# Normalizing x of batches 1 to 3 on ScalarE instead of the vector engine, in a fused attention and mixture-of-experts kernel

## Chip, cores and metric

The kernel runs on one core of one Trainium2 chip. The metric is the device time of one execution in microseconds (us). Engines are named as in the profile: PE is TensorE's matmul, PEld its weight load, DVE is VectorE, ACT is ScalarE, POOL is GpSimd, SP is SyncE.

## The reference, cut to what matters

```python
x = L0_attn_x                                     # (4, 2048, 256) float32
x = x + _layernorm(_L0_attn_ref(_layernorm(x), Wqk, Wv, Wo, tau))
x = x + _layernorm(_L0_ffn_ref(_layernorm(x), ln_g, ln_b, Wr, W1, W3, W2, W1s, W3s, W2s))

def _layernorm(x, eps=1e-5):
    return (x - mean(x)) / sqrt(var(x) + eps)     # over the last axis
def _L0_attn_ref(x, Wqk, Wv, Wo, tau):            # attention over channels
    qk, v = heads_of(x @ Wqk), heads_of(x @ Wv)   # 16 heads of 16 channels, transposed to (b, h, d, n)
    dot = einsum('bhdn,bhen->bhde', qk, qk)
    ...
```

The attention is over channels: its logits come from `dot`, which is Wqk^T (x^T x) Wqk with x the normalized input. So the kernel needs, for each of the 4 batches, one Gram matrix x^T x of 256x256, summed over 2048 tokens. The feed-forward part has one shared expert over all tokens and 7 routed ones, top 2, with a capacity. All is float32.

## The kernel before

**Tiling.** Tokens are cut into 16 groups of 512 (four a batch, `q` = 0 to 3), each held as `[128, GT=4, 256]`. The feed-forward part is a stream of chunks of 512 tokens: `first_chunks()` gives the shared expert's chunks 0 to 13, `routed_chunks` the routed ones, `held_chunks` the last two. Float32 products are made of three fp32r ones: every operand is split into a high part, a rounded copy made by ACT, and a low part, the difference, made by DVE. `three(...)` issues the three matmuls (L1140 to L1142).

**A chunk.** `body` on each engine runs eight steps `m` per chunk. PE: `up` (L1323) makes two products of 512 columns, six matmuls each, into bank 0 and bank 1; `down` for an earlier step (L1345) takes twelve matmuls of 256 columns. ACT: SiLU from bank 0 into `sb_act` (L1063), then the high part of the step before (L1034). DVE: the multiply of bank 1 with `sb_act` (L1738), then the low part (L1714). In chunks 0 to 11 one pair of banks serves: the first six matmuls of the next `up` wait for the SiLU, its other six for the multiply.

**What sets the order.** Each engine has one instruction stream in program order, with semaphores between them. The attention of batches 1 to 3 is threaded by hand into this stream: step m of chunk n has two places, 16n+2m and 16n+2m+1, and `put` enters steps in `schedule` at places. `attend` issues on each engine what that engine has under the step's name (`steps`). On ACT the even place lies behind the SiLU and ahead of the high part, the odd one behind the high part and ahead of the next SiLU. On DVE the even place lies behind the multiply and ahead of the low part, the odd one ahead of the next multiply.

```python
X_STEPS = (("x_stats", 0), ("x_norm", 3), ("x_high", 4), ("x_part", 5))
...
X_AT, M_AT, MIX_AT = (None, 14, 72, 131), (None, 34, 93, 152), (None, 46, 109, 164)
for b in range(1, B):
    ...
    for q in range(GB):
        put(b, X_AT[b] + 4 * q, q, X_STEPS)
```

So `x_norm` stands at places 17, 21, 25, 29 of batch 1, at 75, 79, 83, 87 of batch 2 (odd places), and at 134, 138, 142, 146 of batch 3 (even places).

**The steps around the change.** For group q: `x_stats` on DVE takes mean and variance of `xin` into `mvX` (L1431, L1435, L1449); POOL makes `rstdX` (L780); `x_norm` on DVE (L1451, its instructions L1460) writes (x - mean) * rstd to `xnorm[q % 2]`, which is the tile `sb_xn` or `sb_ln_o`, in four instructions of 256 columns; `x_high` on ACT (L930, L933) writes its high part into `xx` (the tiles `sb_wdn_hi` and `sb_wdn_lo`, idle weight space), `x_part` on DVE (L1565, L1568) its low part; `x_gram` on PE (L1144, L1159) multiplies them. When `xn_ok` rises, SP loads the next tokens into `xin` (L560), or the turned x (L570), which ACT splits in `x_keep` (L939). Other steps in the same stretch: `o_add` on DVE (L1584) adds the attention's result, `u_norm` on DVE (L1608, L1612) normalizes for the router, `u_turn0` and `u_turn1` on ACT (L988) copy transposed rows to `sb_hr`, `prep` copies `sb_hfull` to `sb_h_hi` (L1015).

Of the kernel before, what the change touches and what calls it, by code (L numbers as in the profile page):

```python
# [7 lines left out]
ALU = mybir.AluOpType  # L8
ACT = mybir.ActivationFunctionType
# [7 lines left out]
P = 128  # L17
# [4 lines left out]
OPEN = 4  # L22
# [23 lines left out]
def sandwich_kernel(nc, x_in, Wqk, Wv, Wo, tau, ln_g, ln_b, Wr, W1, W3, W2, W1s, W3s, W2s, x_turned, out):  # L46
# [10 lines left out]
    GT = 4  # L57
# [3 lines left out]
    GB = N // GW  # L61
# [36 lines left out]
    with ExitStack() as ctx:  # L98
        def sb(name, shape, dt=F32):
            return ctx.enter_context(nc.sbuf_tensor("sb_" + name, shape, dt))  # L100

        def sem(name):
            return ctx.enter_context(nc.semaphore(name))
# [39 lines left out]
        xin = sb("xin", [P, 2, GT, D])  # L143
        xn = sb("xn", [P, GT, D])
        ln_o = sb("ln_o", [P, GT, D])
        xnorm = [xn, ln_o]
# [38 lines left out]
        stX = sb("stX", [P, 2, GT, 6])  # L185
        mvX = sb("mvX", [P, 2, GT, 2])
        rstdX = sb("rstdX", [P, 2, GT])
        veX = sb("veX", [P, GB, GT])
        outidx = sb("outidx", [P, NG], U32)
        stB = sb("stB", [P, GT, 6])  # L190
# [69 lines left out]
        a_rstd = sem("a_rstd")  # L260
        xn_ok = sem("xn_ok")
        xn_tile = sem("xn_tile")
        xhi_ok = sem("xhi_ok")
        xlo_ok = sem("xlo_ok")
        xT_in = [sem(f"xT_in{i}") for i in range(GB)]
# [2 lines left out]
        g_done = sem("g_done")  # L268
# [658 lines left out]
        def _(act_e):  # L927
            s = nc.scalar

            def x_high(b, q):  # L930
                act_e.wait_ge(xn_ok, OPEN + b * GB + (q + 1))
                act_e.wait_ge(g_done, OPEN + b * GB + q - 1)
                s.activation(xx[q % 2][:, :, 0, :], xnorm[q % 2][:, :, :], ACT.Copy).then_inc(xhi_ok, 1)  # L933
# [22 lines left out]
            def m_halves(dst, banks, ready, order):  # L956
                def step(b, q):
                    for n, k in enumerate(order):
                        act_e.wait_ge(m_pe, b * MP + ready + n)
                        s.activation(dst[:, k, :], bank[banks[k]][:, 0:D], ACT.Copy).then_inc(m_act, 1)  # L960
                return step
# [11 lines left out]
            def u_keep(k):  # L973
                def step(b, q):
# [10 lines left out]
                    if opens(b, q):  # L985
# [3 lines left out]
                                 scale=gcol[:, k:k + 1], bias=bcol[:, k:k + 1]).then_inc(hT_ok, 1)  # L989
                return step  # L990

            steps = {"x_high": x_high, "x_keep": x_keep, "m_gram": m_gram,
                     "m_keep_t": m_halves(tsb, (5, 4), 2, (1, 0)),
                     "m_exp": m_step(lc[:, :, :], lc[:, :, :], m_dve, 3, ACT.Exp),
                     "m_keep_n": m_halves(tsb, (6, 5), 6, (0, 1)),
# [132 lines left out]
            for t in range(GT // 2):  # L1128
                ins = s.activation(last_y[CLOSE % TY][:, t, :], last_y[CLOSE % TY][:, t, :], ACT.Identity,
                                   scale=t_scale[CLOSE % SLOTS][:, t:t + 1], bias=t_bias[CLOSE % SLOTS][:, t:t + 1])  # L1130
# [293 lines left out]
        def _(dve):  # L1424
            v = nc.vector
# [12 lines left out]
            def x_from(b, q):  # L1438
                return x2[:, q, :, :] if b == 0 and q < 2 else xin[:, q % 2, :, :]
# [11 lines left out]
            def x_norm(b, q):  # L1451
                g = b * GB + q
                dve.wait_ge(a_rstd, g + 1)
                if g < GB + 2:
                    dve.wait_ge(g_done, OPEN + g - 1)
                else:
                    dve.wait_ge(xhi_ok, OPEN + g - GB - 1)
                    dve.wait_ge(xlo_ok, OPEN + g - GB - 1)
                for t in range(GT):
                    ins = v.tensor_scalar(xnorm[q % 2][:, t, :], x_from(b, q)[:, t, :], mvX[:, q % 2, t, 0:1],  # L1460
                                          rstdX[:, q % 2, t:t + 1],
                                          ALU.subtract, ALU.mult)
                    if b == 0 and t < GT - 1:
                        ins.then_inc(xn_tile, 1)
                ins.then_inc(xn_ok, 1)

# [198 lines left out]
            def u_place(b, pair):  # L1665
# [17 lines left out]
                dve.sem_inc(r_slot, 1)  # L1683

            steps = {"x_stats": x_stats, "x_norm": x_norm, "x_part": x_part, "x_low": x_low, "o_add": o_add,
                     "m_turn": m_sum, "m_sym": m_sym, "m_pick": m_pick, "m_logits": m_logits,
                     "m_softmax": m_softmax, "m_low": m_low, "o_stats": o_stats, "o_norm": o_norm,
                     "u_stats": u_stats, "u_norm": u_norm, "u_turn1": first_keep, "u_copy": u_copy, "r_top": r_top, "r_next": r_next,
                     "u_slot": u_slot, "u_place": u_place}
# [175 lines left out]
            for t in range(GT // 2, GT):  # L1865
                ins = v.tensor_scalar(y[:, t, :], y[:, t, :], t_scale[CLOSE % SLOTS][:, t:t + 1], t_bias[CLOSE % SLOTS][:, t:t + 1],
                                      ALU.mult, ALU.add)
# [40 lines left out]
```

## Time and profile before

| | before |
|---|---|
| median of 3 runs | 1089.29 us (1087.91 to 1089.88) |
| the profiled execution's own time | 1087.53 us |
| its span | 1085.8 us |
| PE busy / PEld busy | 1049.2 us (97%) / 958.5 us (88%) |
| DVE busy | 656.1 us (60%) |
| ACT busy | 503.5 us (46%) |
| POOL busy | 390.0 us (36%) |
| TensorE clock granted, mean | 0.993 |

The span is the time from the first to the last instruction of one profiled execution; the execution's own time has some 1.7 us around it. Busy time of an engine is the union of its instructions; matmuls overlap one another, so PE can be busy while it is not at its peak. A timeline row gives an instruction's start, its length, and in brackets how long its engine had been idle before it and what ended that.

### The profile page before, as it was taken

How to read it: one execution, taken by the hardware profiler on the slowest of the kernel's cores; microseconds unless marked ns; L12 is line 12 of the kernel's file. 1: busy time of each engine (PE TensorE's matmuls, PEld its weight loads, DVE VectorE, ACT ScalarE, POOL GpSimd, SP SyncE). 2: the span in 40 equal slices, each digit the busy share in tenths (PEclk: the TensorE clock that was granted, in tenths of full speed). 3: DMA queues.
4: the chain of work that ended last, by engine and by line, in shares of the span. 5: the costliest groups of instructions: out<-in, count | busy, mean ns of one | idle time of the engine just before them, and what ended most of it. 6: DMA issues, size and time to landing. Idle time of an engine off the chain costs nothing.

```text
span 1085.8 us, 19513 instructions
## 1 busy us (share of the span) xinstructions
PE 1049.2 (97%) x6863; PEld 958.5 (88%) x6863; DVE 656.1 (60%) x1714; ACT 503.5 (46%) x895; POOL 390.0 (36%) x347
## 2 busy tenths in 40 slices
PE   7998999999999999999989999999999999999995
PEld 6886888888888988889878899999999999999874
DVE  7768864677754578754786334545545463635686
ACT  4343344443434444443454334554546463645485
POOL 3112661114640114541116731344443343312386
PEclk9999999999999999999999999999999999999998
DMA  8322460242540223461134214524344342333699
GB/s 280 114 98 78 138 214 20 78 157 93 174 142 20 100 96 141 134 221 49 59 136 162 93 43 152 139 62 117 82 96 106 68 124 52 81 79 105 239 237 178
DMA packets 47229, 129.15 MB, mean 119 GB/s; under 512 B 10276, under 2 KB 17576, under 8 KB 47152
## 3 DMA queue, kind: packets, MB, share of 16 engines
q1 hardware_dynamic: 28656, 92.83, 25.1%
q0 software_dynamic: 18496, 35.35, 14.2%
q8 instruction: 43, 0.70, 0.3%
q14 instruction: 34, 0.28, 0.1%
HBM read 73.72 MB, written 54.40 MB: 118 GB/s over the span
## 4 chain that ended last, share of the span: by engine, by line
PE 82%; DVE 8%; POOL 3%; issue 3%; ACT 1%; DMA 1%; DVEq 0%; SPq 0%; POOLq 0%; ACTq 0%
PE bank L1140 25%; PE bank L1142 25%; PE bank L1141 25%; PE bank L1159 3%; POOL out_dram L908 2%; POOL sb_place_of L913 2%; DVE sb_act L1738 1%; PE bank L1266 1%; PE bank L1319 1%; DVE sb_act_lo L1714 1%; PE bank L1219 1%; DVE sb_stX L1431 1%; DVE sb_st L1431 1%; PE bank L1278 1%; ACT sb_ln_o L967 1%
## 5 line engine op out<-in xcount | busy, mean ns | idle before, releaser
L1140 PE MATMUL bank<-sb_h_hi,sb_wup_lo 128*128 128x512 f32 (+2 forms) x960 | 354.4, 369 | 5.3 <-DVE sb_act L1738 3.8
L1738 DVE TENSOR_TENSOR sb_act<-bank,sb_act 128x512 f32<-128x512 f32 (+2 forms) x240 | 148.6, 619 | 345.9 <-PE bank L1142 317.1
L1142 PE MATMUL bank<-sb_h_hi,sb_wup_hi 128*128 128x512 f32 (+2 forms) x960 | 350.0, 365 | 0.0
L1141 PE MATMUL bank<-sb_h_lo,sb_wup_hi 128*128 128x512 f32 (+2 forms) x960 | 349.6, 364 | 0.0
L1063 ACT ACTIVATE sb_act<-bank 128x512 f32<-128x512 f32 (+2 forms) x240 | 129.8, 541 | 354.6 <-PE bank L1142 328.9
L1140 PE MATMUL bank<-sb_wdn_hi,sb_act_lo 128*128 128x256 f32 (+1 forms) x848 | 246.5, 291 | 5.8 <-DVE sb_act_lo L1714 5.8
L1142 PE MATMUL bank<-sb_wdn_hi,sb_act_hi 128*128 128x256 f32 (+1 forms) x848 | 240.1, 283 | 0.0
L1141 PE MATMUL bank<-sb_wdn_lo,sb_act_hi 128*128 128x256 f32 (+1 forms) x848 | 239.9, 283 | 0.0
L1140 PEld LDWEIGHTS bank<-sb_h_hi,sb_wup_lo 128*128 128x128 f32 x960 | 180.5, 188 | 27.2 <-DVE sb_act L1738 6.4
L1142 PEld LDWEIGHTS bank<-sb_h_hi,sb_wup_hi 128*128 128x128 f32 x960 | 180.5, 188 | 22.5
L1141 PEld LDWEIGHTS bank<-sb_h_lo,sb_wup_hi 128*128 128x128 f32 x960 | 180.9, 188 | 17.0
L1140 PEld LDWEIGHTS bank<-sb_wdn_hi,sb_act_lo 128*128 128x128 f32 (+1 forms) x848 | 159.7, 188 | 11.6 <-DVE sb_act_lo L1714 6.9
L1714 DVE TENSOR_TENSOR sb_act_lo<-sb_act,sb_act_hi 128x512 fp32r<-128x512 f32 (+2 forms) x240 | 147.2, 613 | 36.1 <-ACT sb_act_hi L1034 34.8
L1141 PEld LDWEIGHTS bank<-sb_wdn_lo,sb_act_hi 128*128 128x128 f32 (+1 forms) x848 | 159.6, 188 | 3.3
L1142 PEld LDWEIGHTS bank<-sb_wdn_hi,sb_act_hi 128*128 128x128 f32 (+1 forms) x848 | 159.5, 188 | 0.0
L1034 ACT ACTIVATE sb_act_hi<-sb_act 128x512 fp32r<-128x512 f32 (+2 forms) x240 | 136.6, 569 | 0.3 <-DVE sb_act L1738 0.3
L864 POOL DMA_INDIRECT y_scratch<-sb_ysb,sb_scur x42 | 76.9, 1832 | 154.1 <-ACT sb_ysb L1052 87.8
L784 POOL TENSOR_TENSOR sb_rstdB<-sb_veB,sb_mhalf 128x4 f32<-128x4 f32 x16 | 19.0, 1187 | 218.1 <-DVE sb_veB L1557 218.1
L800 POOL DMA_INDIRECT sent_scratch<-sb_rows,sb_sendto x64 | 70.7, 1104 | 28.9 <-issue 19.9
L833 POOL DMA_INDIRECT sb_rows<-sent_scratch,sb_gcur x42 | 44.6, 1063 | 77.3 <-issue 52.5
L788 POOL TENSOR_TENSOR sb_rstd<-sb_ve,sb_mhalf 128x4 f32<-128x4 f32 x16 | 19.8, 1239 | 77.5 <-DVE sb_ve L1593 77.5
L967 ACT ACTIVATE sb_ln_o<-bank,sb_nbiasB,sb_rstdB 128x256 f32<-128x256 f32 x64 | 30.9, 563 | 27.5 <-DVE sb_nbiasB L1562 27.5
(265 smaller groups left out, 1240.6 us busy)
## 6 DMA issues: line engine op xcount, KB each, us to landing
sb_xin<-in_L_ffn_W_dram SPq DMA_DIRECT2D x28, 512.0 KB, 3.5
sb_x<-in_L_attn_x_dram SPq DMA_DIRECT2D x16, 512.0 KB, 3.7
out_dram<-sb_x SPq DMA_DIRECT2D x16, 512.0 KB, 3.5
sb_xin<-in_L_attn_x_dram SPq DMA_DIRECT2D x14, 512.0 KB, 5.1
sb_xin<-in_x_turned_dram SPq DMA_DIRECT2D x14, 512.0 KB, 3.9
y_scratch<-sb_ysb SPq DMA_DIRECT2D x14, 512.0 KB, 3.6
sb_xn<-in_L_ffn_W_dram SPq DMA_DIRECT2D x14, 512.0 KB, 3.9
hT_scratch<-sb_hr SPq DMA_DIRECT2D x12, 512.0 KB
```

Of the source, the lines that this page charges most:

```text
L800: pool.indirect_dma_start(sent_d, bass.IndirectOffsetOnAxis(ap=sendto[:, q, t, c:c + 1], axis=0), u[q][:, t, :], None).then_inc(sent[q], 16)
L833: pool.indirect_dma_start(rows[0:w, part, t, :], None, sent_d, bass.IndirectOffsetOnAxis(ap=gcur[0:w, part, t:t + 1], axis=0)).then_inc(ga ...
L864: pool.indirect_dma_start(y_d, bass.IndirectOffsetOnAxis(ap=scur[0:w, par, part, t:t + 1], axis=0), ysb[0:w, part, t, :], None, compute_op ...
L967: ins = s.activation(ln_o[:, t, :], bank[o_bank(b, q) + t // 2][:, (t % 2) * D:(t % 2 + 1) * D], ACT.Identity, scale=rstdB[:, t:t + 1], bi ...
L1034: s.activation(act_hi[:, m % 4, 0:c.w], act[:, m % 3, 0:c.w], ACT.Copy).then_inc(ahi_ok, 1)
L1063: s.activation(act[:, m % 3, 0:c.w], a[:, 0:c.w], ACT.Silu).then_inc(silu_ok, 1)
L1140: t_.matmul(o, a_lo, b_hi, start=start, stop=False, skip_group_check=True)
L1141: t_.matmul(o, a_hi, b_lo, start=False, stop=False, skip_group_check=True)
L1142: return t_.matmul(o, a_hi, b_hi, start=False, stop=stop, skip_group_check=True)
L1159: ins = t_.matmul(bank[4 + k][:, o:c], a[:, k * P:(k + 1) * P], a[:, o:c], start=(q == 0 and t == 0), stop=(q == GB - 1 and t == GT - 1))
L1714: v.tensor_tensor(act_lo[:, m % 4, 0:c.w], act[:, m % 3, 0:c.w], act_hi[:, m % 4, 0:c.w].bitcast(F32), ALU.subtract).then_inc(alo_ok, 1)
L1738: v.tensor_tensor(act[:, m % 3, 0:c.w], bank[(4 if c.wide and m % 2 else 0) + 1][:, 0:c.w], act[:, m % 3, 0:c.w], ALU.mult).then_inc(act_o ...
```

## The change

On DVE, `x_norm` of batches 1 to 3 no longer writes the normalized tile; it makes the four bias values per partition, -mean * rstd, in one small instruction and signals `x_nb`. On ACT a new `x_norm`, at the same places of the schedule, waits for it and writes the tile by four ACTIVATEs with scale rstd and that bias. Its wait for the tile to be free is the old one (`g_done` or `xlo_ok`); `xhi_ok` is no longer waited for, since `x_high` is earlier on the same engine. Batch 0 is as it was. Instructions per group: DVE loses four of 128x256 and gains one of 128x4, ACT gains four of 128x256; there are 12 groups.

```diff
+        nbX = sb("nbX", [P, 2, GT])
...
+        x_nb = sem("x_nb")
...
+            def x_norm(b, q):
+                if b == 0:
+                    return
+                g = b * GB + q
+                act_e.wait_ge(x_nb, g - GB + 1)
+                if g < GB + 2:
+                    act_e.wait_ge(g_done, OPEN + g - 1)
+                else:
+                    act_e.wait_ge(xlo_ok, OPEN + g - GB - 1)
+                for t in range(GT):
+                    ins = s.activation(xnorm[q % 2][:, t, :], xin[:, q % 2, t, :], ACT.Identity,
+                                       scale=rstdX[:, q % 2, t:t + 1], bias=nbX[:, q % 2, t:t + 1])
+                ins.then_inc(xn_ok, 1)
...
-            steps = {"x_high": x_high, "x_keep": x_keep, "m_gram": m_gram,
+            steps = {"x_norm": x_norm, "x_high": x_high, "x_keep": x_keep, "m_gram": m_gram,
...
             def x_norm(b, q):
                 g = b * GB + q
                 dve.wait_ge(a_rstd, g + 1)
-                if g < GB + 2:
-                    dve.wait_ge(g_done, OPEN + g - 1)
-                else:
-                    dve.wait_ge(xhi_ok, OPEN + g - GB - 1)
-                    dve.wait_ge(xlo_ok, OPEN + g - GB - 1)
+                if b > 0:
+                    v.scalar_tensor_tensor(out=nbX[:, q % 2, :], in0=mvX[:, q % 2, :, 0], scalar=-1.0,
+                                           in1=rstdX[:, q % 2, :], op0=ALU.mult, op1=ALU.mult).then_inc(x_nb, 1)
+                    return
+                dve.wait_ge(g_done, OPEN + g - 1)
                 for t in range(GT):
                     ins = v.tensor_scalar(xnorm[q % 2][:, t, :], x_from(b, q)[:, t, :], mvX[:, q % 2, t, 0:1],
                                           rstdX[:, q % 2, t:t + 1],
                                           ALU.subtract, ALU.mult)
-                    if b == 0 and t < GT - 1:
+                    if t < GT - 1:
                         ins.then_inc(xn_tile, 1)
                 ins.then_inc(xn_ok, 1)
```

How the streams now stand (the lines of the changed kernel are 16 higher from L946 on). ACT in batch 1, from the first group's place on; before, `sb_act<-bank0` is the SiLU, `sb_wdn_hi1` and `sb_wdn_lo1` are `x_high`:

```order
L1034 ACTIVATE sb_act_hi<-sb_act 128x512
L1063 ACTIVATE sb_act<-bank0 128x512
L933 ACTIVATE sb_wdn_hi1<-sb_xn 128x4x256
L1034 ACTIVATE sb_act_hi<-sb_act 128x512
L1063 ACTIVATE sb_act<-bank0 128x512
L1034 ACTIVATE sb_act_hi<-sb_act 128x512
L1045 ACTIVATE sb_ysb<-bank2 128x512
L1045 ACTIVATE sb_ysb<-bank3 128x512
L1063 ACTIVATE sb_act<-bank0 128x512
L933 ACTIVATE sb_wdn_lo1<-sb_ln_o 128x4x256
```

The same stretch now, where `sb_xn<-sb_xin` and `sb_ln_o<-sb_xin` are the new `x_norm`:

```order
L1050 ACTIVATE sb_act_hi<-sb_act 128x512
L942 ACTIVATE sb_xn<-sb_xin,sb_nbX,sb_rstdX 128x256 x4
L1079 ACTIVATE sb_act<-bank0 128x512
L949 ACTIVATE sb_wdn_hi1<-sb_xn 128x4x256
L1050 ACTIVATE sb_act_hi<-sb_act 128x512
L1079 ACTIVATE sb_act<-bank0 128x512
L1050 ACTIVATE sb_act_hi<-sb_act 128x512
L1061 ACTIVATE sb_ysb<-bank2 128x512
L1061 ACTIVATE sb_ysb<-bank3 128x512
L942 ACTIVATE sb_ln_o<-sb_xin,sb_nbX,sb_rstdX 128x256 x4
L1079 ACTIVATE sb_act<-bank0 128x512
L949 ACTIVATE sb_wdn_lo1<-sb_ln_o 128x4x256
```

Four ACTIVATEs now stand directly ahead of a SiLU, in both groups; before, the SiLU stood ahead of everything that needs the normalized tile. DVE at the first of these two places, now (L1600 is `o_add`, L1754 the multiply):

```order
L1730 TENSOR_TENSOR sb_act_lo<-sb_act,sb_act_hi 128x512
L1600 TENSOR_TENSOR sb_x2<-sb_ln_o,sb_x2 128x1024
L1471 SCALAR_TENSOR_TENSOR sb_nbX<-sb_mvX,sb_rstdX 128x4
L1754 TENSOR_TENSOR sb_act<-bank1,sb_act 128x512
L1675 TENSOR_TENSOR sb_place_of<-bank6,sb_carry 128x112
```

The bias stands where the four DVE instructions stood, behind `o_add` and ahead of the multiply. ACT in batch 3 at its first group's place, now:

```order
L1079 ACTIVATE sb_act<-bank0 128x512
L942 ACTIVATE sb_xn<-sb_xin,sb_nbX,sb_rstdX 128x256 x4
L1050 ACTIVATE sb_act_hi<-sb_act 128x512
L1004 ACTIVATE sb_hr<-bank6,sb_bcol,sb_gcol 128x512
L949 ACTIVATE sb_wdn_hi1<-sb_xn 128x4x256
L1079 ACTIVATE sb_act<-bank0 128x512
```

Here the new step stands behind a SiLU; ahead of the next SiLU come the high part, the copy to `sb_hr` and `x_high`, as before, but now all behind the four ACTIVATEs.

## Rows read from the trace of the kernel before

**Rows 1.** The page, busy time of each engine over the span.
```profile
PE 1049.2 (97%) x6863; PEld 958.5 (88%) x6863; DVE 656.1 (60%) x1714; ACT 503.5 (46%) x895; POOL 390.0 (36%) x347
```
**Rows 2.** Waits of PE from 80 to 560 us: us in total, times, longest.
```profile
PE bank L1140 <- DVE sb_act L1738: 3.5, 3, 2.8
...
PE bank L1159 <- DVE sb_wdn_lo L1568: 0.3, 1, 0.3
```
**Rows 3.** Line L1460 from 60 to 560 us: who waited for it (us, times).
```profile
  ACT sb_wdn_lo L933: 12.4, 4
  ACT sb_wdn_hi L933: 7.1, 3
```
**Rows 4.** Timeline of ACT near the end, start and length in us.
```profile
1030.30 1.08 ACT L1114 ACTIVATE sb_xn<-sb_xn,sb_place_of 128x256 f32<-128x256 f32 x2
```
**Rows 5.** Line L1562 of DVE, the bias of another layer norm, ns min/median/max.
```profile
L1562 DVE SCALAR_TENSOR_TENSOR sb_nbiasB<-sb_mvB,sb_rstdB x16: 151/152/161, 40.5 to 546.9; 128x4 f32<-128x4 f32 x16
```
**Rows 6.** Timeline of all engines, batch 1, groups 0 and 1.
```profile
97.40 0.60 ACT L1063 ACTIVATE sb_act<-bank 128x512 f32<-128x512 f32 x1 [0.82 <-DVE sb_act_lo L1714]
...
98.36 1.38 DVE L1460 TENSOR_SCALAR sb_xn<-sb_xin,sb_mvX,sb_rstdX 128x256 f32<-128x256 f32 x4
98.43 0.39 PE L1140 MATMUL bank<-sb_h_hi,sb_wup_lo 128*128 128x512 f32 x1
...
99.65 0.69 DVE L1738 TENSOR_TENSOR sb_act<-bank,sb_act 128x512 f32<-128x512 f32 x1
...
106.89 0.68 DVE L1738 TENSOR_TENSOR sb_act<-bank,sb_act 128x512 f32<-128x512 f32 x1
...
107.62 0.50 PE L1140 MATMUL bank<-sb_h_hi,sb_wup_lo 128*128 128x512 f32 x1 [2.75 <-DVE sb_act L1738]
...
111.59 1.37 DVE L1460 TENSOR_SCALAR sb_ln_o<-sb_xin,sb_mvX,sb_rstdX 128x256 f32<-128x256 f32 x4
...
114.15 0.39 PE L1140 MATMUL bank<-sb_h_hi,sb_wup_lo 128*128 128x512 f32 x1
```
**Rows 7.** Busy time by stretch: PE, PEld, DVE, ACT, POOL, granted clock, DMA share, GB/s.
```profile
104.60:108.00 3.40, 0.65 (x4) 0.34 (x3) 3.19 (x11) 0.60 (x2) 1.91 (x1) 1.00 0.41 165
108.00:111.40 3.40, 3.40 (x13) 2.92 (x12) 3.04 (x10) 0.00 (x0) 1.19 (x1) 0.50 0.01 2
```
**Rows 8.** Timeline of all engines, batch 1, group 3.
```profile
131.21 0.60 ACT L1063 ACTIVATE sb_act<-bank 128x512 f32<-128x512 f32 x1 [3.09 <-PE bank L1142]
...
133.45 1.38 DVE L1460 TENSOR_SCALAR sb_ln_o<-sb_xin,sb_mvX,sb_rstdX 128x256 f32<-128x256 f32 x4
...
137.08 1.22 DVE L1470 TENSOR_TENSOR sb_wup_lo<-sb_xin,sb_wup_hi 128x1024 fp32r<-128x1024 f32 x1
...
138.22 1.22 DVE L1568 TENSOR_TENSOR sb_wdn_lo<-sb_ln_o,sb_wdn_lo 128x1024 fp32r<-128x1024 f32 x1
...
138.75 1.06 ACT L939 ACTIVATE sb_wup_hi<-sb_xin 128x1024 fp32r<-128x1024 f32 x1 [0.46 <-DMA sb_xin<-in_x_turned_dram]
...
140.31 1.81 PE L1159 MATMUL bank<-sb_wdn_lo 128*128 128x512 f32 x8
```
**Rows 9.** Timeline of all engines, batch 2, group 1.
```profile
268.24 1.38 DVE L1460 TENSOR_SCALAR sb_ln_o<-sb_xin,sb_mvX,sb_rstdX 128x256 f32<-128x256 f32 x4
...
270.60 0.69 DVE L1738 TENSOR_TENSOR sb_act<-bank,sb_act 128x512 f32<-128x512 f32 x1 [0.98 <-PE bank L1142]
...
276.39 1.91 PE L1159 MATMUL bank<-sb_wdn_lo 128*128 128x512 f32 x8 [0.26 <-DVE sb_wdn_lo L1568]
```
**Rows 10.** Timeline of all engines, batch 3, group 0.
```profile
418.30 1.38 DVE L1460 TENSOR_SCALAR sb_xn<-sb_xin,sb_mvX,sb_rstdX 128x256 f32<-128x256 f32 x4 [0.25 <-DVE sb_sendto L1680]
...
420.68 0.58 ACT L1063 ACTIVATE sb_act<-bank 128x512 f32<-128x512 f32 x1
...
421.16 0.77 ACT L988 ACTIVATE sb_hr<-bank,sb_bcol,sb_gcol 128x512 f32<-128x512 f32 x1
421.31 0.50 PE L1140 MATMUL bank<-sb_h_hi,sb_wup_lo 128*128 128x512 f32 x1
```

## The prediction

> **What bounds the kernel now.** I read the page first: TensorE is busy for 97% of the span, DVE for 60%, ACT for 46% [rows 1]. So neither DVE nor ACT is short of time on the whole; a shift of work between them counts only where TensorE stands still for one of them. The second view is what TensorE waits for in the stretch with batches 1 to 3: the multiply L1738 holds it 3.5 us in 3 times, 2.8 of them at once, and the low part of normalized x (L1568) holds it 0.3 us in batch 2, group 1 [rows 2]. The third is the line that moves: ACT waited 12.4 + 7.1 = 19.5 us for its result [rows 3]. The last is the timeline at the twelve places, which decides.
>
> **Prices.** DVE loses, per group, four instructions that together take 1.38 us [rows 6], and gains one of 128x4, 0.15 us [rows 5]. ACT gains four ACTIVATEs from SBUF to SBUF, 128x256, with scale and bias per partition. The trace has this form at L1114: two take 1.08 us, and one alone 0.59, so they start 0.49 us apart [rows 4]. Four take 4 x 0.49 = 1.97 us until the next can start (the one alone is estimated as 1.08 - 0.49). The Trainium skill (page "VectorE: DVE Perf Modes", section "The TRN2 errata") has a table that gives ScalarE from SBUF to SBUF 224 + 256 cycles at 1.2 GHz, 0.40 us for one such instruction; by it a group would cost ACT some 1.6 us, each SiLU would be 0.4 us less late, and the sum below about 3.7 us. The rows say 0.59, and the measurement decides.
>
> ACT's 12 x 1.97 = 24 us are more than DVE's 12 x 1.2 = 15 us. Neither total is the change in time. What matters is the order: the four ACTIVATEs wait for DVE's bias, and the SiLU waits behind them, though it needs nothing of them. TensorE's next `up` needs that SiLU in its first six matmuls, and DVE's multiply, which stands right behind the bias, needs it too.
>
> **Batch 1, group 0.** The bias stands where the normalization started, 98.36, so it ends at 98.51. A hand-over takes some 0.05 us: the multiply that ends at 107.57 is followed by its matmul at 107.62 [rows 6]. ACT: 98.55 + 1.97 = 100.52, then the SiLU, 0.60, to 101.12. Before, the SiLU ran at 97.40 and its matmul at 98.43; now that matmul starts at 101.15, 2.7 us later. The multiply, before at 99.65, starts at 101.15 too, 1.5 later. From there to the multiply at 106.89 DVE has no pause (3.19 us busy of 3.40 in the stretch from 104.6, and all that it does there it does one after another [rows 7]), so TensorE's matmul at 107.62, which waits for that multiply, comes **1.5 us later**, not 2.7: DVE was the late one there and gets its own relief of 1.2 back only as a pause.
>
> **Group 1.** Its bias comes on DVE at 111.59 + 1.5 = 113.09. ACT: 113.28 + 1.97 = 115.25, SiLU to 115.85, and the matmul that waits for it at 115.9; before 114.15 [rows 6]. That is **+1.75** in all. The granted clock fell to half speed (1.2 of 2.4 GHz) from 108.0 to 111.4, behind a pause of 2.75 us [rows 7]; the new pause there is shorter (estimated 2.1 us), so the clock may hold. Worth nothing here: at full clock TensorE would be back at about 115.3 and still wait for the SiLU.
>
> **Groups 2 and 3.** Group 2 costs nothing: its SiLU comes late too, but TensorE has the router's matmuls and a Gram product in front of it. Group 3 does cost. Its bias stands at 133.45 behind a full DVE; the SiLU that ran at 131.21 now waits: 133.45 + 1.75 = 135.2, ACT from 135.4 to 137.4, SiLU to 138.0. Behind it on ACT stand the split of turned x (0.96 each, estimated as 1.06 less the overlap), `x_high` (the same) and a high part (0.52), to 140.4. Then DVE makes a low part (0.6), L1470 and L1568 (1.13 each) and ends at 143.4. Before, L1568 ended at 139.44 and the Gram product ran at 140.31 [rows 8]; now it starts at 143.45. So batch 1 costs **+3.1 us**. The DMA of turned x, which starts when the tile is written, is 2.6 us later and lands at about 141.3 instead of 138.75 [rows 8]; ACT's next split waits for it a little, with slack behind.
>
> **Batch 2.** Groups 0 and 2: DVE is not late there, the bias comes while TensorE still fills the SiLU's bank, and ACT's 1.97 us fit ahead of it: 0. Group 1: bias 268.24, ACT to 270.4, SiLU to 271.0, multiply 271.05 instead of 270.60, 0.45 later, and DVE then runs without a pause to L1568, for which the Gram product at 276.39 had waited already [rows 9]: **+0.45**. Group 3 by the same sum: **+0.3**.
>
> **Batch 3.** Even places: the step is behind a SiLU, so the high part comes late first, which has time. But the next SiLU stands behind all of it. Group 0: bias 418.30, ACT 418.5 to 420.46, high part 0.52 (as long as a SiLU, 0.6), copy to `sb_hr` 0.69 (0.77), `x_high` 0.97 (1.06), each less 0.1 of overlap, SiLU 422.64 to 423.22, matmul 423.27 instead of 421.31 [rows 10], nearly 2.0, of which some 0.25 are had back, since the next six matmuls had waited for DVE before. **+1.7**. Groups 1 to 3 together **+0.3** (the multiply behind group 2 comes late).
>
> **Where relief is.** The stalls that a freer DVE could shorten are those of rows 2. In the sum it shortens none, since each DVE queue has its multiply behind a SiLU that is later by more than DVE gains. I cost at nothing: the new semaphore, the dropped wait for `xhi_ok`, and SP's loads (the tile is done up to 2.6 us later; what they load is needed a group's step later). POOL has no new work.
>
> **Sum.** 3.1 + 0.75 + 2.0 = 5.85 us on the profiled execution's own 1087.53 us: 1093.4. The median of the runs is 1.76 us above that execution; 1089.29 + 5.85 gives **1095.1 us**. Bounds: the lower is what only the three first-order delays give, 1.5 + 1.7 = 3.2, less the scatter of the runs (1.4): 1091. The upper adds the clock (below).
>
> **Rivals.**
> 1. *The clock falls twice more.* TensorE would now stand for some 2.6 us at 98.6 and 2.0 us at 421.2; a pause of 2.75 us was followed by 3.4 us at half speed, which costs 1.7 us [rows 7]. Price up to 3.4 us on top: 1098.5. Against it: in batch 1 DVE's queue sets the end anyway.
> 2. *Faster: DVE is what TensorE waits for.* The mechanism is one: at 106.89 the multiply comes 1.2 us earlier, the pause of 2.75 us becomes 1.5, the clock does not fall (1.7 us), the 0.4 of the first multiply and the 0.6 of L1568 go: about 4.5 us, 1084.8. For it: DVE ends nearly all of TensorE's waits here [rows 2]. It decides at one point: whether the bias is made before the SiLU could run. At 98 us the SiLU could run at 97.40 and the bias comes at 98.51 [rows 6]; at 131 it is 2.2 us before the bias [rows 8]. Only batch 2 has it the other way.
> 3. *No change: it fits in the time in which ACT waited.* ACT sat 19.5 us idle for this tile [rows 3] and now writes it itself; if TensorE's slack took the late SiLUs, the time stays 1089.3. For it: groups 0 and 2 of batch 2. Against: in batch 1 and 3 the matmul had 0.4 us or less behind the SiLU [rows 6, 10]: it ended at 98.00 and was used at 98.43.
> That the change does not do what it says can be left out: the streams show it.
>
> The Trainium skill (page "ScalarE: Activation LUTs", section "Rules for kernel authors") says to put additions and multiplications on VectorE, not ScalarE; the rows agree per instruction, 0.49 against 0.33 us apart, but by that rule alone the price would be 24 - 15 = 9 us, which no row supports, since neither engine is full.
>
> **How the numbers follow.** The forecast has 0.69, the clock rival 0.12, no change 0.10, faster 0.09. The range reaches from 1091.0 to 1099.0: the two rivals on the slower side are in it, the other two (0.19) are out. A measurement of this kernel tells 0.2%, 2.2 us, from no change. The forecast's own lower bound is above that, so slower has 0.69 + 0.12 = 0.81, within 0.2% 0.10, faster 0.09.
>
> **What would show it.** In the profile after: ACT's four ACTIVATEs start 0.2 us behind DVE's bias at some 98.5, 113.3, 135.4 and 420, with a SiLU right behind or behind three more; TensorE then has new waits for ACT's SiLU L1079 of about 2.6 us at 98.6, 0.5 at 115, 2.0 near 423, and one of 1 us for L1584 near 142. DVE's busy time falls by 15 us, ACT's rises by 24, ACT's waits of 19.5 us for the tile are gone. It is wrong if the SiLU at 98 us is not late, if four ACTIVATEs take far from 2 us, or if a stall at 107 us became shorter than 1.6 us.

## The result and the profile after

| | before | after | after, repeated |
|---|---|---|---|
| median of the runs beside each other | 1088.97 us | 1097.16 us (1095.79 to 1099.97) | 1096.01 us (1095.08 to 1096.82), before 1087.33 |
| ratio to before, 95% interval | | 1.0094 (1.0075 to 1.0113) | 1.0086 (1.0073 to 1.0099) |
| span of the profiled execution | 1085.8 us | 1098.2 us | 1093.3 us |

The change makes the kernel slower, by 8.2 us between the medians of the first comparison and by 8.7 in the second. The first ratio, 1.0094, is more than the medians of that comparison give (1.0075); in the second the two agree within 0.1%. On the 1089.29 us of the forecast the first ratio gives 1099.5 us, the second 1098.7. The forecast was +5.85 us and 1095.1, its range 1091.0 to 1099.0: the direction is right, the size is too small by a third (of 8.7 us) or more (10.2 us by the first ratio), and the first ratio's value lies just over the range.

On the page after, the numbers of instructions have moved as the streams say [rows 1 for before]: DVE has 36 fewer and is busy for 13.8 us less, ACT has 48 more and is busy for 23.0 us more.

```profile
span 1098.2 us, 19525 instructions
PE 1051.8 (96%) x6863; PEld 960.0 (87%) x6863; DVE 642.3 (58%) x1678; ACT 526.5 (48%) x943; POOL 386.6 (35%) x347
```

The costliest groups of ACT, apart by form, hold the new line. It has two rows, one for each buffer of normalized x:

```profile
L942 ACT ACTIVATE sb_ln_o<-sb_xin,sb_nbX,sb_rstdX 128x256 f32<-128x256 f32 x24 | 12.5, 590 | 23.4 <-DVE sb_nbX L1471 23.4
L942 ACT ACTIVATE sb_xn<-sb_xin,sb_nbX,sb_rstdX 128x256 f32<-128x256 f32 x24 | 12.5, 590 | 12.1 <-DVE sb_nbX L1471 12.1
```

ACT used to wait 19.5 us for DVE's finished tile [rows 3]; now it waits 35.5 us for DVE's bias, and everything behind it on ACT waits too. What TensorE waited for between 80 and 570 us (engine, what it waited for: us in total, times, the longest), to be held against [rows 2]:

```profile
PE bank L1156 <- ACT sb_act L1079: 6.4, 5, 2.6
PE bank L1156 <- DVE sb_act L1754: 2.5, 2, 2.1
PE bank L1205 <- DVE sb_u L1513: 2.1, 2, 1.0
PE bank L1175 <- DVE sb_wdn_lo L1584: 2.0, 2, 1.1
PE bank L1282 <- DVE sb_early L1628: 1.0, 1, 1.0
```

The waits for ACT's SiLU (L1079) are new but for 1.3 us, and so is most of the wait for the low part of x (L1584, before L1568). The timeline of batch 1, group 0, shows how the first arises: ACT, then DVE, then TensorE (start, length, instruction, and in brackets the idle time before it with what ended it).

```profile
98.05 0.64 ACT L1050 ACTIVATE sb_act_hi<-sb_act 128x512 fp32r<-128x512 f32 x1
100.65 2.07 ACT L942 ACTIVATE sb_xn<-sb_xin,sb_nbX,sb_rstdX 128x256 f32<-128x256 f32 x4 [1.97 <-DVE sb_nbX L1471]
102.63 0.57 ACT L1079 ACTIVATE sb_act<-bank 128x512 f32<-128x512 f32 x1
```

```profile
98.72 0.69 DVE L1730 TENSOR_TENSOR sb_act_lo<-sb_act,sb_act_hi 128x512 fp32r<-128x512 f32 x1 [2.52 <-ACT sb_act_hi L1050]
99.33 1.22 DVE L1600 TENSOR_TENSOR sb_x<-sb_ln_o,sb_x 128x1024 f32<-128x1024 f32 x1
100.46 0.15 DVE L1471 SCALAR_TENSOR_TENSOR sb_nbX<-sb_mvX,sb_rstdX 128x4 f32<-128x4 f32 x1
103.24 0.69 DVE L1754 TENSOR_TENSOR sb_act<-bank,sb_act 128x512 f32<-128x512 f32 x1 [2.62 <-ACT sb_act L1079]
```

```profile
103.26 0.50 PE L1156 MATMUL bank<-sb_h_hi,sb_wup_lo 128*128 128x512 f32 x1 [2.57 <-ACT sb_act L1079]
```

ACT is free at 98.7, DVE's bias comes at 100.6 behind a residual addition (L1600) that has nothing to do with it, the SiLU stands behind the four ACTIVATEs, and DVE then stands for 2.62 us for that SiLU. Each engine waits for the other in turn, and though neither is busy, TensorE's matmul comes 2.8 us later than before (103.26 for 98.43, less the 2.0 us that are explained next).

One part of the profiled difference of 12.4 us isn't the change's. In the first execution TensorE's matmuls start 2.0 us later than before's from 37 us on, ahead of every instruction that was changed. The repetition has nothing of it; there they start 0.6 us earlier than before's. The granted clock of the same stretch in the two, first execution and repetition (columns: us, busy time of PE, PEld, DVE, ACT, POOL, PEclk, DMA share, GB/s):

```profile
34.30:37.70 3.40, 3.40 (x18) 2.95 (x17) 2.08 (x4) 2.15 (x4) 0.00 (x0) 0.50 0.00 0
```

```profile
34.30:37.70 3.40, 3.22 (x27) 3.21 (x27) 3.40 (x7) 1.19 (x2) 0.00 (x0) 1.00 0.00 0
```

### The profile page after: what moved, and what is told of

The parts are those of the page before. It is cut to its first block, busy times and chain, and to the rows that moved or that the text cites. A ratio compares the mean times of both kernels' runs of the same rounds, so it can differ in the third digit from the quotient of the medians.

```text
span 1098.2 us, 19525 instructions
## 1 busy us (share of the span) xinstructions
PE 1051.8 (96%) x6863; PEld 960.0 (87%) x6863; DVE 642.3 (58%) x1678; ACT 526.5 (48%) x943; POOL 386.6 (35%) x347
## 4 chain that ended last, share of the span: by engine, by line
PE 76%; DVE 12%; issue 4%; POOL 3%; ACT 3%; DMA 1%; DVEq 0%; POOLq 0%; ACTq 0%; SPq 0%
PE bank L1156 24%; PE bank L1158 23%; PE bank L1157 23%; PE bank L1175 2%; POOL out_dram L910 2%; POOL sb_place_of L915 2%; DVE sb_act L1754 1%; DVE sb_stX L1447 1%; DVE sb_act_lo L1730 1%; PE bank L1282 1%; PE bank L1335 1%; DVE sb_st L1447 1%; PE bank L1235 1%; ACT sb_ln_o L983 1%; DMA sb_ysb<-in_L_ffn_W2s_dram 1%
## 5 line engine op out<-in xcount | busy, mean ns | idle before, releaser
L1754 DVE TENSOR_TENSOR sb_act<-bank,sb_act 128x512 f32<-128x512 f32 (+2 forms) x240 | 148.6, 619 | 357.3 <-PE bank L1158 311.5
L1079 ACT ACTIVATE sb_act<-bank 128x512 f32<-128x512 f32 (+2 forms) x240 | 129.6, 540 | 326.8 <-PE bank L1158 300.5
L1050 ACT ACTIVATE sb_act_hi<-sb_act 128x512 fp32r<-128x512 f32 (+2 forms) x240 | 136.5, 569 | 0.3 <-DVE sb_act L1754 0.3
L983 ACT ACTIVATE sb_ln_o<-bank,sb_nbiasB,sb_rstdB 128x256 f32<-128x256 f32 x64 | 30.9, 563 | 28.8 <-DVE sb_nbiasB L1578 28.8
```

Of the source, the lines that this page charges most:

```text
L983: ins = s.activation(ln_o[:, t, :], bank[o_bank(b, q) + t // 2][:, (t % 2) * D:(t % 2 + 1) * D], ACT.Identity, scale=rstdB[:, t:t + 1], bi ...
L1050: s.activation(act_hi[:, m % 4, 0:c.w], act[:, m % 3, 0:c.w], ACT.Copy).then_inc(ahi_ok, 1)
L1079: s.activation(act[:, m % 3, 0:c.w], a[:, 0:c.w], ACT.Silu).then_inc(silu_ok, 1)
L1754: v.tensor_tensor(act[:, m % 3, 0:c.w], bank[(4 if c.wide and m % 2 else 0) + 1][:, 0:c.w], act[:, m % 3, 0:c.w], ALU.mult).then_inc(act_o ...
```

## The experiments

Every kernel ran in 5 rounds beside the kernel before on its chip (before's medians: 1086.74 us in the first series, 1087.33 and 1087.39 in the others). Effects below are differences of medians; the intervals are of the ratio, and the two need not agree (for dve_signal 5.6 us and 4.5 us). Two theories stood against each other. **Order**: the loss comes from where the ACTIVATEs and the bias stand in two queues that wait for each other. **Engine time**: it comes from 24 us of added ACT work.

| kernel | median | effect | ratio, 95% interval |
|---|---|---|---|
| act_time | 1086.31 us | -0.4 | 0.9991 (0.9981 to 1.0002) |
| bias_only | 1087.86 | +1.1 | 1.0006 (0.9996 to 1.0015) |
| pool_bias | 1086.32 | -0.4 | 0.9997 (0.9987 to 1.0008) |
| behind_silu | 1090.55 | +3.8 | 1.0029 (1.0017 to 1.0040) |
| after_again | 1096.01 | +8.7 | 1.0086 (1.0073 to 1.0099) |
| only_b1 | 1091.00 | +3.7 | 1.0040 (1.0025 to 1.0055) |
| only_b3 | 1091.34 | +4.0 | 1.0039 (1.0027 to 1.0051) |
| bias_early | 1087.86 | +0.5 | 1.0005 (0.9994 to 1.0016) |
| dve_signal | 1092.97 | +5.6 | 1.0041 (1.0026 to 1.0056) |
| behind_silu_b3 | 1090.19 | +2.8 | 1.0018 (1.0006 to 1.0031) |
| before_late | 1088.08 | +0.7 | 1.0005 (0.9993 to 1.0018) |
| pool_late | 1087.24 | -0.2 | 0.9998 (0.9985 to 1.0011) |

### The ACTIVATEs alone, the wait alone

act_time is the kernel before with four ACTIVATEs of the same form per group at the new places on ACT, waiting for nothing of DVE's:

```diff
+            def x_norm(b, q):
...
+                for t in range(GT):
+                    ins = s.activation(xx[q % 2][:, t, 0, :], wo[:, t % 2, :], ACT.Identity,
+                                       scale=mhalf[:, 0:1], bias=mhalf[:, 1:2])
```

> The kernel before, DVE normalizing as before, and on ACT at the places of x_norm four ACTIVATEs of the same form on constant data that nothing waits for, with no wait for a bias. Order theory: ACT has the time free where it stands, the SiLU is late by 0.75 us at most, +0 to +1 us over before. Engine-time theory (24 us more on ACT are the price): +4 us or more.

bias_only is the changed kernel with the four ACTIVATEs left out:

```diff
-                for t in range(GT):
-                    ins = s.activation(xnorm[q % 2][:, t, :], xin[:, q % 2, t, :], ACT.Identity,
-                                       scale=rstdX[:, q % 2, t:t + 1], bias=nbX[:, q % 2, t:t + 1])
-                ins.then_inc(xn_ok, 1)
+                act_e.sem_inc(xn_ok, 1)
```

> The changed kernel, but ACT's x_norm only waits for the bias and signals; its four ACTIVATEs are left out, so x of batches 1 to 3 is not normalized (the Gram products take old data). Order theory (the cost is that each SiLU stands behind the bias and the 1.97 us of ACTIVATEs): the SiLU at 98 us is then late by 0.75 us only and the multiply behind it early by 0.45, so the time is that of the kernel before or some 1 us less, 1086 to 1089.5. Coupling theory (the wait for the bias alone costs most of it): 1092 or more.

Both run within 0.2% of before. The 48 ACTIVATEs cost nothing, so engine time falls; the waits for the bias alone cost little too (0.6 to 1.1 us, not clear of the scatter). Only the two together cost 8 us: the ACTIVATEs fit into ACT's idle time if they may run when ACT gets there, and don't when they begin late.

### The bias from another queue

In pool_bias GpSimd makes the bias right behind rstd, which it makes anyway; ACT's part is the changed kernel's, place for place.

```diff
+                if b > 0:
+                    pool.wait_ge(a_rstd, b * GB + (q + 1))
+                    v.tensor_tensor(nbX[:, q % 2, :], mvX[:, q % 2, :, 0], rstdX[:, q % 2, :], ALU.mult).then_inc(x_nb0, 1)
+                    pool.wait_ge(x_nb0, (b - 1) * GB + (q + 1))
+                    v.tensor_scalar(nbX[:, q % 2, :], nbX[:, q % 2, :], -1.0, None, ALU.mult).then_inc(x_nb, 1)
```

> The changed kernel with the bias made by POOL right behind rstd (two small instructions), so that ACT's x_norm stands at the same places but does not wait for DVE's queue. Order theory: only the 1.97 us on ACT are left ahead of the SiLU, the matmul at 98 us is 0.75 us late instead of 2.7, batch 1 costs 0 to 1 us, in all -1 to +2 us against before. Engine-time theory: as the change, +8 us.

The loss is gone. The same groups of ACT and the timeline of GpSimd and ACT at batch 1, group 0:

```profile
L948 ACT ACTIVATE sb_ln_o<-sb_xin,sb_nbX,sb_rstdX 128x256 f32<-128x256 f32 x24 | 12.4, 591 | 3.3 <-POOL sb_nbX L788 3.3
L948 ACT ACTIVATE sb_xn<-sb_xin,sb_nbX,sb_rstdX 128x256 f32<-128x256 f32 x24 | 12.4, 592 | 0.6 <-POOL sb_nbX L788 0.6
```

```profile
94.05 0.25 POOL L788 TENSOR_SCALAR sb_nbX<-sb_nbX 128x4 f32<-128x4 f32 x1
...
96.66 2.08 ACT L948 ACTIVATE sb_xn<-sb_xin,sb_nbX,sb_rstdX 128x256 f32<-128x256 f32 x4
98.63 0.59 ACT L1085 ACTIVATE sb_act<-bank 128x512 f32<-128x512 f32 x1
```

The bias is there at 94.3, and ACT has the SiLU at 98.63 instead of 102.63 (100.6 without the 2.0 us of the opening). It also shows what the relief of DVE is worth here: ACT does the whole normalization, DVE is 14.6 us less busy than before (641.5 against 656.1), and the time is before's; the interval leaves room for a gain of 1.4 us.

### One place earlier on DVE

bias_early leaves ACT as changed and only lets DVE make the bias one place sooner.

```diff
-        X_STEPS = (("x_stats", 0), ("x_norm", 3), ("x_high", 4), ("x_part", 5))
+        X_STEPS = (("x_stats", 0), ("x_bias", 2), ("x_norm", 3), ("x_high", 4), ("x_part", 5))
```

> The whole change, but DVE makes the bias one place earlier in its order (about 1.5 us of its queue), ahead of that place's other work; ScalarE's four ACTIVATEs stay where they are. If what costs is how late the bias comes out of DVE's queue, the waits of ScalarE for the bias (36 us in all in the changed kernel) fall by a third or more and most of the loss goes: +1 to +4 us over before instead of +8. If a bias by DVE costs by its being DVE's at all, or if the ACTIVATEs' own 1.97 us per group are what delays the SiLU, it stays at +7 us or more.

It runs within 0.2% of before: of 8.7 us, 0.5 are left. Its groups of ACT and DVE's timeline:

```profile
L942 ACT ACTIVATE sb_ln_o<-sb_xin,sb_nbX,sb_rstdX 128x256 f32<-128x256 f32 x24 | 12.5, 591 | 14.2 <-DVE sb_nbX L1471 14.2
L942 ACT ACTIVATE sb_xn<-sb_xin,sb_nbX,sb_rstdX 128x256 f32<-128x256 f32 x24 | 12.5, 592 | 4.3 <-DVE sb_nbX L1471 4.3
```

```profile
94.06 0.15 DVE L1471 SCALAR_TENSOR_TENSOR sb_nbX<-sb_mvX,sb_rstdX 128x4 f32<-128x4 f32 x1
96.66 0.69 DVE L1730 TENSOR_TENSOR sb_act_lo<-sb_act,sb_act_hi 128x512 fp32r<-128x512 f32 x1 [2.45 <-ACT sb_act_hi L1050]
```

The one place was worth much more than the 1.5 us I had put to it: between the two places DVE stands 2.45 us for ACT's high part (L1050). A bias behind that wait is late by the wait as well: it comes at 94.06 here and at 98.46 in the changed kernel (100.46 less 2.0). ACT still waits 18.5 us for the bias in all, about what it waited for the tile before, and the time is only 0.5 us over before's. behind_silu (below) waits only 10.8 us (7.4 + 3.4) and loses 3.8. So the sum of an engine's waits doesn't rank the cost; what stands behind them does.

### An empty signal in the bias's place

dve_signal is pool_bias, with ACT also waiting for a signal that DVE gives where the changed kernel makes the bias. DVE computes nothing.

```diff
                 if b > 0:
+                    dve.sem_inc(x_go, 1)
                     return
...
                 act_e.wait_ge(x_nb, g - GB + 1)
+                act_e.wait_ge(x_go, g - GB + 1)
```

> GpSimd makes the bias right behind rstd, as in pool_bias, which ran at before's time; but ScalarE waits, ahead of its four ACTIVATEs, for an empty signal that DVE gives at the place in its order where the changed kernel's DVE makes the bias. DVE computes nothing for x here. If the loss is the place in DVE's order and nothing else, this kernel loses as the changed one does: +8 to +9 us over before, with TensorE's pauses of 2.5 us at 101 us, 0.9 at 143, 1.1 at 280 and 1.9 at 427. If the loss came of the small instruction that computes the bias, or of ScalarE reading what DVE has just written, it stays within 2 us of before.

+5.6 us by the medians, 4.5 by the ratio (2.8 to 6.1): half to two thirds of the loss, without any work. Group 0 of batch 3 loses what it lost in the change: TensorE's waits for the SiLU are

```profile
PE bank L1164 <- ACT sb_act L1087: 4.0, 3, 1.8
```

of which 1.84 at 424.6. A half clock of 3.4 us at 425.5, which the repetition of the change doesn't have, costs some 1.2 us more. What I missed is mostly in batch 1: over it TensorE falls behind before's start times by 0.9 us here and by 3.3 in the change (over batch 2 by 0.4 and 1.2). In its group 0 ACT starts at 96.84, before DVE's addition begins, where in the change the bias came only after that addition:

```profile
96.84 2.08 ACT L950 ACTIVATE sb_xn<-sb_xin,sb_nbX,sb_rstdX 128x256 f32<-128x256 f32 x4 [0.25 <-issue]
```

```profile
96.62 0.69 DVE L1737 TENSOR_TENSOR sb_act_lo<-sb_act,sb_act_hi 128x512 fp32r<-128x512 f32 x1 [2.52 <-ACT sb_act_hi L1058]
97.23 1.22 DVE L1607 TENSOR_TENSOR sb_x<-sb_ln_o,sb_x 128x1024 f32<-128x1024 f32 x1
```

So a bare signal isn't a stand-in for an instruction at the same place: by 96.84 it had left DVE, when the low part ahead of it was still running and the addition was still to start. The kernel is a clean test of the place for batch 3, group 0, and not for batch 1; for batch 1 bias_early is the test.

### Behind the SiLU instead of ahead of it

behind_silu calls the ACTIVATEs at the head of `x_high`, one place later on ACT; in batches 1 and 2 this is behind the SiLU.

```diff
             def x_high(b, q):
+                x_norm(b, q)
...
-            steps = {"x_norm": x_norm, "x_high": x_high, "x_keep": x_keep, "m_gram": m_gram,
+            steps = {"x_high": x_high, "x_keep": x_keep, "m_gram": m_gram,
```

> The changed kernel with ACT's x_norm moved down one place, directly ahead of x_high: in batches 1 and 2 it then stands behind the SiLU, in batch 3 behind the high part and the copy to sb_hr, still ahead of the next SiLU. Same instructions on every engine. Order theory: batches 1 and 2 cost nothing and give back up to 1.5 us (DVE's relief at 98 to 107 us), batch 3 costs 0.75 us: 1087 to 1090.5. Engine-time theory: as the change, 1095 or more.

Batch 1 is healed. Up to 500 us the pauses of TensorE that are left over before's are three: 0.35 at 276.2 and 1.18 at 298.4 (batch 2, the low part of x, which now comes late), 0.8 at 423.6 (batch 3). The expectation had batch 2 at nothing. behind_silu_b3 moves batch 3 one place further:

```diff
-            steps = {"x_high": x_high, "x_keep": x_keep, "m_gram": m_gram,
+            steps = {"x_high": lambda b, q: b < 3 and x_high(b, q),
+                     "x_part": lambda b, q: b == 3 and x_high(b, q), "x_keep": x_keep, "m_gram": m_gram,
```

> behind_silu cost +3.1 us, and its trace has TensorE pauses grown by 0.8 us at 423.6 us (batch 3, where ScalarE's normalization still stood ahead of the next SiLU) and by 0.4 and 1.2 us in batch 2 (276 and 298 us). Here batch 3's stands one place later, behind the next SiLU. If the order against the SiLU is what costs, the pause at 423.6 us goes back to 0.1 us and the time falls to +2 to +2.5 us over before, the rest being batch 2's; if the later place makes a Gram product late instead, a new pause of 0.5 us or more stands in front of a product of x in batch 3, and the time stays at +3 or goes over it.

The pause at 423.6 went, and one of 0.39 for the low part appeared at 426.1; the gain (1.0 us by the medians measured beside before) is inside the intervals. A later place for the ACTIVATEs trades a late SiLU for a late Gram product.

### Batch by batch

> The changed kernel once more, beside the kernels of this series. Its first profiled execution was 12.4 us slower in its span than before's, of which 2.0 us arose at 32 to 36 us, ahead of anything that the change touches, behind a weight load that landed late, and 1.3 us came from a clock fall at 430.3 us. If the 2.0 us are scatter and the clock fall belongs to the change, this execution has no loss at 32 us and again a half clock of 3.4 us behind TensorE's pause at about 428 us, and the median is 8 to 9 us over before's. If the clock fall is scatter too, the median lies 6 to 7 us over before's. If the opening's loss belongs to the change, the median lies 10 us or more over.

> The change in batch 1 alone; batches 2 and 3 are normalized by DVE as before. The sum on record gives batch 1 +3.1 us, the changed kernel's trace +3.3: so +3 to +3.5 us over before, with pauses of about 2.6 us at 101 us and 2.1 us at 109 us and 0.9 us at 143 us. If the loss were not local but came of the engine time of all 48 ACTIVATEs, this one would cost a third of the whole change, 2.7 us, which the time alone can't tell apart, but then no pause of TensorE would have grown at these three places.

> The change in batch 3 alone. By the sum on record +2.0 us; if the pause of 1.9 us at its first group brings the clock down for 3.4 us, as in the changed kernel's trace, +1.8 for the pause, +1.3 for the clock and +0.7 for group 2: +3.8 us. A trace without a half clock between 420 and 430 us, with the time at +2 to +2.5 us, would say that the fall belongs to what batches 1 and 2 left behind.

Both single-batch kernels pick their batches by a list:

```diff
-                if b == 0:
+                if b not in MOVED:
                     return
...
-                if b > 0:
+                if b in MOVED:
                     v.scalar_tensor_tensor(out=nbX
```

Batch 1 alone costs 3.7 us, batch 3 alone 4.0, and of the 8.7 of both with batch 2 one us is left for it; batch 2 alone was not run. TensorE's start times, held against before's matmul for matmul, test this better than the medians. Over batch 1 they fall behind by 3.3 us in only_b1 and by 3.3 in the repetition, so batch 1's loss doesn't hang on the others. Over batch 3 they fall behind by 3.9 us in only_b3, 1.2 of them by a half clock, and by 2.3 in the repetition: 2.7 and 2.3 without the clock.

The repetition lost nothing at 32 us and had no half clock at 428 us, and its median is still 8.7 us over before's; the expectation had tied 8 to 9 us to that half clock.

The clock does not explain the loss of the profiled executions. Batch 3 alone had a clock fall behind its pause of 1.93 us, and so had the first execution of the whole change behind 1.94 us; the repetition had a pause of 1.95 us at the same place and no fall. Windows behind the pause in only_b3 and in the first execution, then two of the repetition (the second is the same place; columns as above):

```profile
425.10:428.50 3.40, 3.40 (x20) 2.26 (x22) 1.93 (x3) 0.60 (x1) 2.62 (x3) 0.50 0.65 258
```

```profile
430.30:433.70 3.40, 3.40 (x9) 2.63 (x9) 2.72 (x8) 1.52 (x3) 2.42 (x3) 0.50 0.87 343
```

```profile
102.00:105.40 3.40, 3.40 (x11) 2.75 (x10) 3.22 (x14) 1.21 (x3) 1.31 (x1) 0.50 0.95 311
427.60:431.00 3.40, 3.40 (x28) 2.42 (x28) 3.15 (x9) 1.60 (x3) 2.38 (x2) 1.00 0.93 376
```

Between 80 and 600 us the kernel before had two stretches of 3.4 us at half clock (108.0, 568.8), the change two (430.3, 580.4), its repetition two (102.0, 576.5). They moved; they did not become more. A fall did cost about 1.2 us where it came (TensorE's start times went from 2.36 to 3.55 us behind before's in only_b3, from 8.78 to 10.00 in the first execution). Of the executions without a profile only the mean granted clock is on record: its median is 0.990 in the repetition's five and 0.992 in before's seventeen beside them. One fall of 3.4 us lowers the mean by 0.0016 (an estimate: half of 3.4 in 1090 us), so one fall more in the median execution, some 1.2 of the 8.7 us, can't be ruled out.

### Is there more to be had at the largest pause?

The largest pause of before, 2.75 us at 107.62, ends with a multiply that stands behind the low part of x [rows 6]. before_late and pool_late put that multiply first:

```diff
-                put(b, X_AT[b] + 4 * q, q, X_STEPS)
+                put(b, X_AT[b] + 4 * q, q, X_STEPS if (b, q) != (1, 0) else X_STEPS[:3] + (("x_part", 6),))
```

> The kernel before, with one step moved: DVE's subtraction for the low part of x of batch 1's first group (1.22 us, 105.75 to 106.97 us) goes behind the up multiply that it stands ahead of. TensorE's pause of 2.75 us ended with that multiply, so it falls to about 1.5 us: -1.2 us; if the half clock at 108.0 us then doesn't come, up to 1.7 us more, -2.9 us. If something else is due just then (the Gram product of that low part, or the routing's place numbers behind it), less than 0.5 us comes back.

> pool_bias with the same move of one subtraction in batch 1. If the two are independent: before's time less the gain of before_late, -1 to -3 us. DVE is there free of the multiplications of x (25 us over the kernel), so if that relief is worth anything once the pause at 107 us is shorter, this one is the faster of the two; if the relief is worth nothing, they are the same within 1 us.

Neither is faster than before, where -1 us or more was expected. In before_late the pause is shorter and the clock stays up, and then TensorE stands for DVE's normalized rows 5 us later, a wait that before did not have:

```profile
106.22 0.50 PE L1140 MATMUL bank<-sb_h_hi,sb_wup_lo 128*128 128x512 f32 x1 [1.62 <-DVE sb_act L1738]
111.55 0.66 PE L1266 MATMUL bank<-sb_ident,sb_early 128*128 128x128 f32 x4 [2.25 <-DVE sb_early L1612]
```

Against before, TensorE gained 1.13 us by the shorter pause and 1.5 us by the full clock behind it, and lost 2.4 of these 2.6 us at the new wait. In before, half clock filled that time. In pool_late the pause is 0.96 us and the new wait 1.88 us. No version here beats the kernel before clear of the scatter.

## Why the prediction was right in kind and short in size

**The steps of batch 1 held to a tenth.** Less the 2.0 us of the opening, the matmul behind group 0's SiLU came at 101.26 (forecast 101.15), the one behind DVE's multiply 1.6 us late (1.5), group 1's at 115.99 (115.9), and group 3's Gram product at 143.60 (143.45): +3.3 us for batch 1 against the 3.1 of the sum. only_b1 gives 3.7 by the medians. Four ACTIVATEs took 2.08 us to their end and 1.98 to the SiLU's start, as priced from L1114 [rows 4]. One took 0.59 us in the mean of all 48; 0.40 us, the estimate from the errata table (the Trainium skill, page "VectorE: DVE Perf Modes", section "The TRN2 errata"), is 0.19 us too short.

One sign of being wrong, a stall at 107 us of less than 1.6 us, came up in the repetition (0.56 us at 108.64; 2.09 in the first execution). It was a poor sign: the half clock at 102.0 had slowed the matmuls ahead of the stall, and the matmul behind it was 1.5 us late, as forecast.

**The clock.** A fall fewer was argued to be worth nothing in batch 1: TensorE would wait for the SiLU anyway. That held; the fall of before at 108.0 did not come in the first execution, and TensorE then stood 1.03 us for L1628 and 0.35 for the SiLU.

**What was too small.** The mechanism was right; the step that failed is the sum. It had batch 2, group 1 at 0.45 us (0.8 measured) and groups 1 to 3 of batch 3 at 0.3 (0.7), and it left out everything behind 500 us without a reason (0.8). The range's upper end allowed for a clock rival and not for these. Held against the repetition's start times of TensorE, matmul for matmul:

| part | forecast | repetition |
|---|---|---|
| batch 1 | +3.1 | +3.3 |
| batch 2 | +0.75 | +1.2 |
| batch 3 | +2.0 | +2.3 |
| behind 500 us | 0 | +0.8 |

Batch 2, group 1, was "0.45 later, and DVE then runs without a pause": the multiply came 0.45 late, but the low part 0.8, since DVE has a pause of 0.26 us behind its statistics that it did not have. Group 3 of batch 2 made 0.4 for 0.3. In batch 3 group 0 gave 1.84 us, less 0.26 that came back: 1.6 for the forecast's 1.7. "Groups 1 to 3 together +0.3" gave 0.7. TensorE's pause for the multiply behind group 2 is 0.44 us alone, since DVE had stood 2.67 us for ACT's high part earlier in its queue (first execution):

```profile
449.69 0.69 DVE L1730 TENSOR_TENSOR sb_act_lo<-sb_act,sb_act_hi 128x512 fp32r<-128x512 f32 x1 [2.67 <-ACT sb_act_hi L1050]
```

The 0.8 us behind 500 us, where no instruction is moved, I had not counted at all. About 0.2 of it is a pause for ACT's L983 at 527.7, another 0.24 a longer pause at 576.3 (2.41 for 2.17). Both stand in every trace in which ACT waits for a bias or a signal of DVE in batch 2, bias_early and bias_only among them, and in none of the others (only_b1, only_b3, act_time, pool_bias, pool_late, before_late). So they go with the change; how they come from it is open, and so is what they are worth, since bias_early has them at 0.5 us over before. The four parts make 7.6 us; 0.4 more lie between them in steps of about 0.1. The rest of the gap, from 8.0 in the trace to 8.7 by the medians, is within the scatter of the runs.

The lower end of the range is said to hold three first-order delays, and adds two (1.5 and 1.7).

**ACT's waits.** "ACT's waits of 19.5 us for the tile are gone" was right in its words and missed the point: they came back as 35.5 us for the bias (33.6 in the repetition). The forecast looked at the bias as 0.15 us of work and priced its place only where TensorE followed at once.

**The rivals.** *The clock twice more* did not happen. One of the two pauses that it named was followed by a fall in each execution (430.3 in the first, 102.0 in the repetition), but before's fall at 108.0 came in neither, and a fall cost some 1.2 us, not 1.7. *Faster through DVE's relief* fell with pool_bias, which has the relief without the loss and gains nothing clear of the scatter, and with before_late, which shortens the pause that it was priced on and gains nothing. Its turning point, whether the bias is made before the SiLU could run, was the right one. *No change* fell for this order of the steps, and is what bias_early and pool_bias do. By engine time (24 - 15 = 9 us, from the busy times) the total would have been nearly hit, for a wrong reason: act_time has all of ACT's added time and DVE's full load, and runs at before's time. The Trainium skill (page "ScalarE: Activation LUTs", section "Rules for kernel authors") says to put additions and multiplications on VectorE, not ScalarE, and gives no such sum. pool_bias does those of 12 groups on ACT, and its time is before's.

## What to carry to other kernels

When work moves from one in-order queue to another, the small instruction that stays behind (here a bias of 128x4, 0.15 us) carries the place of the old queue with it: whoever waits for it waits for everything ahead of it, and everything behind the waiter waits too. Put such a value where its inputs are made, or one place ahead of the queue's next wait, before judging the move; here that turned +8.7 us into -0.4 and +0.5, neither clear of the scatter. And an engine that is 60% busy and ends TensorE's waits isn't thereby short of time: taking 14 us off it gained nothing that the runs can tell.

## What the runs showed of the hardware

- The same pause, at the same place, of the same kernel (1.94 and 1.95 us before batch 3's matmul) was followed by 3.4 us at 1.2 GHz in one execution and by full clock in the other; the stretch at 102.0 in the repetition has no like in the first. At another place, the pause of 2.2 to 2.4 us that ends at 569 us in before, the clock fell in seven of the fourteen traces (in before, both of the change, only_b1, dve_signal, bias_only and pool_late). So such a pause by itself doesn't settle whether the clock falls, what does isn't shown, and one profile can't price it.
- A bare semaphore signal in DVE's stream had gone out by 96.84 us, with the vector instruction ahead of it running until 97.31 and one that was due before it starting only at 97.23; in the changed kernel an instruction at the same place went behind both.
- Half clock can cost next to nothing: in the kernel before, TensorE ran at half clock from 108.0 to 111.4 us, DVE's normalized rows (L1612) were done at 111.68, and TensorE started on them at 112.08, at most 0.4 us later than it could have.
